# Second cross attention, top-32 selection: where the softmax is normalised, and which engine selects the second head

## The reference, cut to what matters

```
Q = (x_text @ Wq).reshape(Bb, Tt, H, DH)            # H = 4, DH = 32, Tt = 256
K = (x_vision @ Wk).reshape(Bb, Gg, H, DH)          # Gg = 4096
scores = jnp.einsum('bthd,bghd->bhtg', Q, K) / np.sqrt(DH)
scores = jnp.where(vision_mask[:, None, None, :], scores, -jnp.inf)
topv, topi = jax.lax.top_k(scores, K_TOP)           # K_TOP = 32
probs = jax.nn.softmax(topv, axis=-1)
attn = jnp.zeros_like(scores).at[bi, hi, ti, topi].set(probs)
attn_mean = attn.mean(axis=1)                       # mean over the 4 heads
c_t = jnp.einsum('btg,bgd->btd', attn_mean, V)      # V = x_vision @ Wv, applied later
```

## Time and profile before

| | |
|---|---|
| median of 3 runs | 2086.05 us (2084.93 to 2088.73) |
| the profiled execution | 2084.4 us, span of its trace 2082.6 us |
| mean granted clock of TensorE | 0.88 of full |
| busy over the span | PE 84%, DVE 58%, ACT 49%, POOL 36% |
| stage of the change | about 1141 us (first statistics on DVE) to 1720.5 us (last CS) |

### The profile page before, as it was taken

One profiled execution on the slowest core, in us unless ns is written; L12 is line 12 of the kernel. 1 busy time (PEld: TensorE's weight loads), 2 busy tenths in 40 slices (PEclk: granted clock), 3 DMA queues, 4 the chain that ended last, 5 costly groups with the idle time before them and its releaser, 6 DMA issues.

```text
span 2082.6 us, 34689 instructions
## 1 busy us (share of the span) xinstructions
PE 1755.0 (84%) x13676; PEld 1114.9 (54%) x13676; DVE 1214.4 (58%) x2969; ACT 1025.3 (49%) x1391; POOL 753.6 (36%) x660
## 2 busy tenths in 40 slices
PE   6889999999999998888788868777777658987884
PEld 3445655565565555565577325344553455776663
DVE  5154241415333202636784698999999967547776
ACT  2578578667766991211311545546565521114542
POOL 6364334414533400000300076978779721110001
PEclk9999999999999998999788557788886779999987
DMA  7865649655664712000100003122231251000000
GB/s 153 168 114 125 136 110 139 136 117 123 131 129 102 112 61 80 2 1 2 54 1 6 9 16 86 52 85 76 69 93 37 74 189 68 0 1 1 1 6 16
DMA packets 80061, 150.01 MB, mean 72 GB/s; under 512 B 15464, under 2 KB 65448, under 8 KB 73480
## 3 DMA queue, kind: packets, MB, share of 16 engines
q1 hardware_dynamic: 64304, 101.80, 17.1%
q0 software_dynamic: 12336, 41.41, 12.9%
q10 hardware_dynamic: 3240, 4.35, 0.8%
HBM read 93.59 MB, written 2.62 MB: 46 GB/s over the span
## 4 chain that ended last, share of the span: by engine, by line
PE 62%; DVE 23%; POOL 4%; ACT 4%; issue 3%; DMA 2%; ACTq 0%; DVEq 0%; POOLq 0%; SPq 0%
PE R L112 37%; PE B L112 22%; DVE CA L1731 5%; DVE PM L1776 5%; PE B L178 2%; POOL ACC L1857 2%; DVE CA L1743 1%; DVE T L1745 1%; ACT PS L2415 1%; ACT PM L1661 1%; DMA CN<-in_ctxn 1%; DMA KST<-OV 1%; DVE MX L2571 1%; POOL PM L1855 1%; DVE A L1067 1%
## 5 line engine op out<-in xcount | busy, mean ns | idle before, releaser
L629 ACT ACTIVATE P<-R 128x1024 f32<-128x1024 f32 x512 | 500.8, 1028 | 128.0 <-PE R L112 113.7
L112 PE MATMUL R<-QS,KST 100*128 100x256 bf16 x2048 | 270.7, 275 | 13.0 <-issue 7.4
L112 PE MATMUL B<-P,VP 128*32 128x256 f32 x4096 | 277.4, 387 | 1.4 <-issue 1.1
L112 PEld LDWEIGHTS R<-QS,KST 100*128 100x128 bf16 x2048 | 182.0, 98 | 138.5 <-issue 64.6
L1857 POOL TENSOR_TENSOR ACC<-ACC,PM 128x4096 f32<-128x4096 f32 x22 | 195.1, 8869 | 1.8
L200 POOL TENSOR_TENSOR LNrs<-LNve,pk_const 128x2 f32<-128x2 f32 x36 | 25.3, 703 | 445.6 <-DVE LNve L196 445.3
L112 PE MATMUL R<-OV,QT 32*128 32x512 f32 x512 | 179.2, 786 | 0.0
L837 POOL DMA_DIRECT2D KST<-OV x300 | 144.5, 490 | 66.5 <-PE R L112 46.4
L112 PEld LDWEIGHTS B<-P,VP 128*32 128x32 f32 x4096 | 107.7, 109 | 102.5 <-issue 33.8
L1847 POOL TENSOR_TENSOR SM<-SM,NG 128x1 f32<-128x1 f32 x30 | 79.3, 2643 | 144.2 <-DVE PM L1776 144.2
L659 DVE CAST OV<-RT 128x512 bf16<-128x512 f32 x64 | 31.4, 490 | 168.4 <-ACT RT L116 99.7
(11 more groups left out here) (346 smaller groups left out, 3374.1 us busy)
## 6 DMA issues: line engine op xcount, KB each, us to landing
KST<-OV POOLq DMA_DIRECT2D x276, 128.0 KB, 10.7
CT<-in_ctxP SPq DMA_DIRECT2D x40, 768.0 KB, 4.8
CN<-in_ctxn SPq DMA_DIRECT2D x60, 384.0 KB, 3.4
CT<-in_ctxT SPq DMA_DIRECT2D x64, 192.0 KB, 2.5
KST<-OV SPq DMA_DIRECT2D x84, 128.0 KB, 8.9
KST<-in_ctxP ACTq DMA_DIRECT2D x4, 768.0 KB, 8.0
pk_a<-in_pk_a SPq DMA_DIRECT2D x1, 3014.0 KB, 9.7
OV<-in_pk_x1b SPq DMA_DIRECT2D x1, 2944.5 KB, 9.9
```

Source lines behind the costliest of these rows:

```text
L112: return e.matmul(o, l, r, start=st, stop=sp, skip_group_check=True)
L629: e.activation(P[(32 * p + k0) % 3][:, :], ring.at(("s", p, k0))[:, :], ACT.Exp).then_inc(*EX.up((p, k0)))
```

## The change

What it does, part by part:

- ACT: `weigh` grows from one instruction to four. A small exponential of the 32 largest candidates with a running sum (into LSUM), a natural logarithm of four times that sum, a subtraction that makes a new bias (negated maximum less logarithm), and the large exponential with that bias: what it writes is already divided by four times the row's sum. `weigh(n-1, 0)` now stands after chunk 5 of block n, and `weigh(p, 1)` at the front of block p + 2, behind `turned` and `done` and ahead of all score copies. It now waits for the flag step of `top`, the last one, where it waited for the maximum before.
- DVE: of the two selects of a pair the first stays, without its sum; the second is gone, except for the last pair. The check and the select stand after the 16th MAX8 in every block, where in even blocks they stood after the 32nd. The reciprocals of `add` are gone and its four additions become two.
- POOL per pair: a comparison of the second head's scores with the 32nd largest (`MK`, bf16), a product of PB with it, and an addition of that to PA. Powers and scalings are gone.
- PE: a query half's two pairs stay in two tiles (four tiles PA, two in use by the transposes at a time), and each 128 x 128 block is transposed from both, the second added to the first in PSUM: 8 matmuls per group where 4 stood.
- The tile of SC is freed by `mask`, `sel(p, 0)` and the second exponential. PB is one tile, so `weigh(p, 1)` waits for the sum of pair p-1. The scratch that GpSimd's transfers use in SBUF is set to 4096 bytes.

The diff, cut to its core:

```
-            PM = [sbt(c, f"PM{i}", [128, NK]) for i in range(3)]
-            ACC = [sbt(c, f"ACC{i}", [128, NK]) for i in range(2)]
+            PA = [sbt(c, f"PA{i}", [128, NK]) for i in range(4)]
+            PB = sbt(c, "PB", [128, NK])
+            MK = sbt(c, "MK", [128, NK], BF16)
...
             def summed(p, k):
-                return V.at(("sum", p, 1, k)) if by_vector(p, 1) else G.at(("sum", p, 1))
+                return V.at(("sum", p, k)) if p == NP - 1 else G.at(("sum", p))
...
                  def turn(m, g):
...
+                    if g == 0:
+                        e.wait_ge(*summed(2 * m, 1))
                     if g % 4 == 0:
                         e.wait_ge(*summed(2 * m + 1, g // 4))
                     for i in range(4):
-                        ins = tr(e, ps[:, i * 128:i * 128 + 128], ACC[m % 2][:, (4 * g + i) * 128:(4 * g + i) * 128 + 128])
+                        for p in (2 * m, 2 * m + 1):
+                            ins = e.matmul(ps[:, i * 128:i * 128 + 128], PA[p % 4][:, (4 * g + i) * 128:(4 * g + i) * 128 + 128], ident,
+                                           start=p == 2 * m, stop=p > 2 * m, is_transpose=True, skip_group_check=True)
...
                 def weigh(p, h):
-                    i = 2 * p + h
-                    if i >= 3:
-                        e.wait_ge(*G.at(("sum", *divmod(i - 3, 2))))
-                    e.wait_ge(*V.at(("nm", p, h)))
-                    e.activation(PM[i % 3][:, :], SC[p % 2][:, h, :], ACT.Exp, bias=SM[p % 3][:, h, NMAX:NMAX + 1], scale=RS).then_inc(*S.up(("e", p, h)))
+                    sm = SM[p % 3][:, h, :]
+                    e.wait_ge(*V.at(("fl", p, h)))
+                    e.activation(TE[:, :], T8[p % 2][:, h, 0:32], ACT.Exp, bias=sm[:, NMAX:NMAX + 1], scale=RS, accum_out=sm[:, LSUM:LSUM + 1]).then_inc(*S.up())
+                    e.wait_ge(*S.now())
+                    e.activation(sm[:, LSUM:LSUM + 1], sm[:, LSUM:LSUM + 1], ACT.Ln, scale=4.0).then_inc(*S.up())
+                    e.wait_ge(*S.now())
+                    e.activation(sm[:, BIAS:BIAS + 1], sm[:, LSUM:LSUM + 1], ACT.Identity, bias=sm[:, NMAX:NMAX + 1], scale=-1.0).then_inc(*S.up())
+                    if h == 0 and p >= 4:
+                        e.wait_ge(*M.at(("t", (p - 4) // 2, 7)))
+                    if h == 1 and p >= 1:
+                        e.wait_ge(*G.at(("sum", p - 1)))
+                    e.wait_ge(*S.now())
+                    e.activation(weights(p, h), SC[p % 2][:, h, :], ACT.Exp, bias=sm[:, BIAS:BIAS + 1], scale=RS).then_inc(*S.up(("e", p, h)))
...
                 def copy(p, ch):
                     if ch == 0 and p >= 2:
-                        e.wait_ge(*V.at(("sel", p - 2, 1)))
+                        e.wait_ge(*V.at(("sel", p - 2, 0)))
+                        e.wait_ge(*G.at(("mask", p - 2)))
+                        e.wait_ge(*S.at(("e", p - 2, 1)))
...
                     if m is not None and gs[3] == 7:
                         done(m)
+                    if 0 <= n - 2 < NP:
+                        weigh(n - 2, 1)
                     for ch in range(8):
...
-                        if ch in (3, 6) and 0 <= n - 1 < NP:
-                            weigh(n - 1, ch // 6)
+                        if ch == 5 and 0 <= n - 1 < NP:
+                            weigh(n - 1, 0)
...
                 def select(p, h):
-                    pm = PM[(2 * p + h) % 3]
-                    e.scalar_tensor_tensor(pm[:, :], ..., ALU.is_ge, ALU.mult, accum_out=SM[p % 3][:, h, SUM:SUM + 1]).then_inc(*V.up(("sel", p, h)))
+                    e.wait_ge(*S.at(("e", p, h)))
+                    e.scalar_tensor_tensor(weights(p, h), SC[p % 2][:, h, :], T8[p % 2][:, h, 31:32], weights(p, h), ALU.is_ge, ALU.mult).then_inc(*V.up(("sel", p, h)))
...
-                            if h == 0 and g == (31 if n % 2 == 0 else 15) and 0 <= n - 2 < NP:
+                            if h == 0 and g == 15 and 0 <= n - 2 < NP:
                                 check(n - 2)
                                 select(n - 2, 0)
-                                select(n - 2, 1)
...
+                for p in range(NP - 1):
+                    pa, pb = weights(p, 0), weights(p, 1)
+                    e.wait_ge(*V.at(("sel", p, 0)))
+                    e.wait_ge(*G.now())
+                    e.tensor_scalar(MK[:, :], SC[p % 2][:, 1, :], T8[p % 2][:, 1, 31:32], None, ALU.is_ge).then_inc(*G.up(("mask", p)))
+                    e.wait_ge(*S.at(("e", p, 1)))
+                    e.wait_ge(*G.now())
+                    e.tensor_tensor(pb, pb, MK[:, :], ALU.mult).then_inc(*G.up(("product", p)))
+                    e.wait_ge(*G.now())
+                    e.tensor_tensor(pa, pa, pb, ALU.add).then_inc(*G.up(("sum", p)))
...
-    nc = _bacc.Bacc("TRN2", target_bir_lowering=False, num_devices=1)
+    nc = _bacc.Bacc("TRN2", target_bir_lowering=False, num_devices=1, dynamic_dma_scratch_size=4096)
```

More of the change, by code:

```diff
@@ L1494, in stage_x1a @@
             SM = [sbt(c, f"SM{i}", [128, 2, 4]) for i in range(3)]
-            ON1, NG1 = sbt(c, "ON1", [128, 1]), sbt(c, "NG1", [128, 1])
+            TE = sbt(c, "TE", [128, 32])
+            ON1 = sbt(c, "ON1", [128, 1])
             ONB = sbt(c, "ONB", [128, 128], BF16)
@@ L1502, in stage_x1a @@
             RS = float(1.0 / np.float64(np.float32(np.sqrt(32.0))))
-            FLAG, NMAX, SUM, REC = range(4)
+            FLAG, NMAX, LSUM, BIAS = range(4)
             NP = 4 * NB
             M, S, V, G = sig("x1_product"), sig("x1_copy"), sig("x1_select"), sig("x1_sum")
-            QV, MRV, GI = sig("x1_query"), sig("x1_mask_row"), sig("x1_pool_set")
+            QV, MRV = sig("x1_query"), sig("x1_mask_row")
             LM1, MUL, MRD = dsig("text_mask"), dsig("x1_mask"), dsig("x1_mask_rows")
@@ L1758, in check @@
                     e.wait_ge(*V.now())
-                    e.wait_ge(*S.at(("e", p, 1)))
                     if "v" not in reg:
@@ L1772, in check @@
                             e.drain()
+                            total = t8[:, h, 33:34]
+                            e.scalar_tensor_tensor(weights(p, h), sc[:, h, :], 0.5, weights(p, h), ALU.is_ge, ALU.mult, accum_out=total)
+                            e.drain()
+                            e.tensor_scalar(total, total, 4.0, None, ALU.mult)
+                            e.drain()
+                            e.reciprocal(total, total)
+                            e.drain()
+                            e.tensor_scalar(weights(p, h), weights(p, h), total, None, ALU.mult)
+                            e.drain()
                 def select(p, h):
-                    pm = PM[(2 * p + h) % 3]
-                    e.scalar_tensor_tensor(pm[:, :], SC[p % 2][:, h, :], T8[p % 2][:, h, 31:32], pm[:, :], ALU.is_ge, ALU.mult,
-                                           accum_out=SM[p % 3][:, h, SUM:SUM + 1]).then_inc(*V.up(("sel", p, h)))
+                    e.wait_ge(*S.at(("e", p, h)))
+                    e.scalar_tensor_tensor(weights(p, h), SC[p % 2][:, h, :], T8[p % 2][:, h, 31:32], weights(p, h), ALU.is_ge, ALU.mult).then_inc(*V.up(("sel", p, h)))
                 def add():
                     p = NP - 1
-                    sm, acc = SM[p % 3], ACC[1]
-                    for h in range(2):
-                        rc = sm[:, h, REC:REC + 1]
-                        e.wait_ge(*V.at(("sel", p, h)))
-                        e.tensor_scalar(rc, sm[:, h, SUM:SUM + 1], 4.0, None, ALU.mult).then_inc(*V.up())
-                        e.wait_ge(*V.now())
-                        e.reciprocal(rc, rc).then_inc(*V.up())
-                    e.wait_ge(*G.at(("sum", p - 1, 1)))
+                    select(p, 1)
+                    e.wait_ge(*V.now())
                     for k in range(2):
                         part = slice(k * NK // 2, (k + 1) * NK // 2)
-                        for h in range(2):
-                            e.wait_ge(*V.now())
-                            e.scalar_tensor_tensor(acc[:, part], PM[(2 * p + h) % 3][:, part], sm[:, h, REC:REC + 1], acc[:, part], ALU.mult, ALU.add).then_inc(*V.up(("sum", p, h, k)))
+                        e.tensor_tensor(weights(p, 0)[:, part], weights(p, 0)[:, part], weights(p, 1)[:, part], ALU.add).then_inc(*V.up(("sum", p, k)))
                 def stats(n, a0, a1):
@@ L1878, in context_in @@
                     elif g < 5:
-                        e.wait_ge(*V.at(("sel", NP - 2, 1)))
+                        e.wait_ge(*G.at(("mask", NP - 2)))
                     else:
```

26 lines of the change are left out of this document (2 added, 24 removed).

## The result

The changed kernel takes 2188.84 us (median of 4 runs, 2181.32 to 2191.36) against 2087.39 us of the kernel before (4 runs, 2084.93 to 2096.1): the ratio is 1.0472, 95% interval 1.0432 to 1.0512. It is slower, as forecast, but by 98 us and not by 31: 2188.84 lies above the range's upper end of 2150.

The account below looks back on a forecast made before the run. ACT was to become the bound in place of DVE, at 35.1 us a block; laid out by position, the stage ends at 1751.5, 31 us later, so 2084.4 + 31 = 2115 us, range 2082 to 2150.

Parts of the forecast that it names:

- 1.4 elsewhere: Time added per four blocks for PE at half clock, outside six copies (3.9) and two turns (2.2): 1.4 us.
- DVE's select, 68.4 us off DVE: On DVE, 15 pairs lose one select of 4.48 us plus 0.08 for its sum's readout: 68.4 us.
- `weigh` at 7.2 us: On ACT, one `weigh` grows from 3.71 to 7.2 us with two table loads of 1.28; bounds 6.9 and 7.8.
- the rival of draining: On ACT, each of 64 table loads costs 1.38 us more for draining: 88 us on top, 2200 us; chance 0.04.
- Full clock: Rival: ACT is the bound with PE's clock full, 133.0 us for four blocks: 2089 us; chance 0.18.
- DVE's pace: Rival: DVE keeps setting the pace, at 27.5 us a block: 2028 us; chance 0.14.
- Per pair POOL has 3.68 + 2 x 8.87 = 21.4 us: POOL's work per pair: mask 3.68 us, product and addition 8.87 each, 21.4 in all.
- SC is freed by `mask`, 4.5 + 3.7 us after the select starts, about as late as now: The SC tile comes free after select (4.5 us) and mask (3.7), about as late as in the kernel before.
- POOL is the ring: Rival: every select falls into a POOL product, lengthening each even block's front by 4.5 us: 32 us, 2147; chance 0.08.
- 140.5 for four blocks: ACT's time for four blocks: 133.0 us at full clock plus half-clock additions, 140.5, or 35.1 each.
- 156 for four blocks: Upper bound of ACT's four blocks, with half of all PE-limited pieces slow: 156 us, adding 43 us to the forecast.
- The tail: From ACT's last score copy at 1674.0 to the stage's end at 1751.5, including the last pair's work.

Follow-up runs that it names:

- mask_mult_mult: The changed kernel with POOL's mask instruction multiplying by the threshold and then by 1.0, not comparing (second head's weights wrong): 2158.27 us, ratio 1.0348.
- mask_dve_weigh_first: The changed kernel with the mask on DVE, one table load, and odd blocks' second-head `weigh` ahead of the turn's four copies: 2077.85 us, ratio 0.9908.

## Why the prediction was wrong

The direction and most durations held; the size did not: 2188.84 is 74 us above 2115. Two terms of the sum were too small, the mask of 3.68 us (about 30 of the 74 us) and the "1.4 elsewhere" for a slow PE (most of the other 43). That ACT's row sets the pace held in part: with its longer `weigh` ACT is busy 64% of the stretch, not the 70 to 75% forecast, and of its 137 us idle some 98 are waits for PE and 24.6 waits for the mask. Going through its steps:

**DVE's select, 68.4 us off DVE: right.** One select of 4.485 us a pair is left. DVE is busy 66%, so here it has slack; no run puts the second select back, so what it is worth by itself is not shown.

**`weigh` at 7.2 us: right (7.3).** No draining was seen, so the rival of draining falls. With one load it is 4.8, inside the 4.6 to 5.9 given for that. **Full clock: wrong** (0.72). **DVE's pace: wrong.**

**"Per pair POOL has 3.68 + 2 x 8.87 = 21.4 us": failed.** The mask was priced by a TENSOR_SCALAR of the same size, but with another pair of operators; it took 10.6. The product, at 7.95 and not 8.87, was a little cheaper; the earlier trace rows, read as a bf16 operand that costs nothing, has its bf16 in the output and fp32 in both inputs.

**"SC is freed by `mask`, 4.5 + 3.7 us after the select starts, about as late as now": failed with it.** It is 4.5 + 10.6, and the copies of even blocks wait (4.83 us above; 24.6 us of ACT's idle time before copies into S in the stretch, in five waits that are gone in mask_mult_mult). In blocks 9 to 12 the mask costs 163.5 - 154.9 = 8.6 us, 6.5 of them in block 10. In the whole kernel that is some 30 us (24 once the loads are gone). The rival "POOL is the ring" named the right engine with the wrong place: not PE waiting for POOL's sum (2.7 us at a time, twice in the stretch), but ACT waiting for POOL's mask.

**"1.4 elsewhere", and so 140.5 for four blocks: failed, and this is the larger part.** With the mask at its forecast price the four blocks 9 to 12 still took 154.9, near the upper bound of 156, and blocks 5 to 8 took 159.8, above it. I had put the half clock on the six copies of the block n % 4 = 1 only. By kind, forecast and measured in mask_mult_mult: 39.1 and 43.3, 32.7 and 29.1, 37.3 and 45.7, 30.0 and 36.8. In the forecast the blocks with keys are 8.4 and 6.8 us too short. ACT in one of them (block 7 there), between its two `weigh`, and then PE:

```profile
1396.89 1.94 ACT L116 ACTIVATE SC<-R 128x1024 f32<-128x1024 f32 x2 [0.17 <-DVE T L1763]
...
1402.47 1.02 ACT L116 ACTIVATE SC<-R 128x1024 f32<-128x1024 f32 x1 [1.11 <-PE R L112]
1406.17 0.60 ACT L116 ACTIVATE OV<-B 128x512 f32<-128x512 f32 x1 [2.68 <-PE B L112]
...
1414.26 0.60 ACT L116 ACTIVATE OV<-B 128x512 f32<-128x512 f32 x1 [2.68 <-PE B L112]
```

```profile
1391.24 1.99 PE L112 MATMUL R<-CT,pk_x1a 96*128 96x256 f32 x8
1397.97 0.61 PE L112 MATMUL R<-OV,ONB 1*128 1x512 bf16 x2 [4.75 <-ACT SC L116]
...
1402.35 3.78 PE L112 MATMUL B<-CT,pk_x1a 96*128 96x256 f32 x8
```

Six copies and three keys take 1396.89 to 1414.86, 18.0 us; the forecast had 9.7, from a key product of 1.99 and chunks 1.09 apart. PE stood idle for 4.75 us behind `weigh`, was then granted half the clock (0.50 from 1398 to 1425 us, though it is busy all the time), and a key product takes 3.78 and a chunk 2.13. So behind a `weigh` comes a slow catching up, in which ACT waits for PE, and the forecast had it in one kind of block only. Shorter `weigh` alone do not cure it: with the loads gone the four blocks are 142.8, not the 140.5 - 20.5 = 120.0 of my sum. A move of `weigh` to where ACT waits anyway pays (blocks n % 4 = 1 in mask_dve_weigh_first). What the clock costs by itself, without the wait ahead of it, no run here isolates, and neither does one the wait for the flag.

**The front of the block n % 4 = 1**, 12.3 us forecast: 1475.97 to 1491.14 in the changed kernel, 15.2, since the first AT copy waits 3 us for a PE that still does the chunks and products of the block before.

**The tail**, 77.5 us from the last copy: 69.9, within 8 us; the second `weigh` of pair 15 did start right behind CS (1790.04).

**The range** had 156 for four blocks as its end, but with "some given back"; that end, taken whole, gave 2158, what mask_mult_mult took. That the two agree is in part chance. By position that run's stage ends 42.1 us behind the forecast's: 7.3 from its start, which differs from run to run, 9.4 in blocks 1 to 4, 34.8 in blocks 5 to 15 (where 156 for four gives 43), and 9.4 less in the tail. The price of the mask I had not bounded at all: I took it from one row.
